# A graph transformer on one core: attention's loop over groups of rows, written out in all five engines

## The chip, the core and the metric

One core of one Trainium2 chip. The time is that of the device, in microseconds (us), of one execution. The core has five engines with an instruction stream each: PE (TensorE, matmuls and their weight loads, which the profile calls PEld), DVE (VectorE), ACT (ScalarE), POOL (GpSimd) and SP (SyncE, which issues the DMAs here). They meet only through semaphores.

## The reference

```python
h = relu(layernorm(x))                                   # x: 1250 x 512, f32
for i in range(4):                                       # L = 4 blocks
    y = cond_layer_norm(h, cond, s1_w[i], ...)
    q, k, v = (y @ wq + bq) * 128 ** -0.5, y @ wk + bk, y @ wv + bv      # 4 heads of 128
    scores = einsum('ehd,ehd->eh', q[src], k[dst])       # 21250 edges
    attn = softmax of the scores over the edges of each src node
    h = h + segment_sum(attn * v[dst], src) @ wo + bo
    y = cond_layer_norm(h, cond, s2_w[i], ...)
    h = h + relu(y @ m_w1 + m_b1) @ m_w2 + m_b2
x = x + h
# then two graph convolutions (GCN) over the same edges with 512 x 512 weights, added to x
```

## The kernel before

The edges are turned at the start into a dense 1250 x 1250 table of counts and a table of its logarithms, the edge bias, kept in memory. Attention is then dense: for a tile of 125 nodes and one head, scores against all 1250 nodes, plus bias, softmax, times V.

The 1250 rows are ten tiles of T = 125, and two tiles make one of NC = 5 **groups**, 0 to 4. A group has UNITS = 8 **units**: 4 heads times 2 tiles, numbered k = 0 to 7. All five engines run a pipeline that is two units deep:

- PE, `unit(G, k)`: `scores` for unit n = k + 2 (9 matmuls into the one score area `ps_S`), then `turn_probs` for unit k (10 transposes of the softmax's output, L1530). After it comes half of `attend` (15 matmuls with V) when k is 2 to 7, all of the last head's (30 matmuls) after k = 0, and `attn_project` (24 matmuls with wo) after k = 1. `scores` waits for two semaphores: `qg` (q is there) and `ttr` (DVE has read the previous unit's scores out of `ps_S`).
- DVE, `unit`: `score_max` for unit n (L1128: one pass of 125x1250 that adds the bias, writes `P` and leaves the row's maximum in `nmx`), `turn_low` for unit k (3 subtractions, L1144), `normalise` for unit n (L1133, L1135 and the scaling L1137). `score_max` waits for three semaphores: `S` (scores are made), `st0` or `st1` (the bias has landed) and `Tp` (PE has transposed the unit before the previous one, so that `P` is free). After odd k comes `out_low` (L1150), and after k = 1 `attn_add` (L1157).
- ACT: exponentials (L757) and copies of the transposes (L763). POOL: splits the next group's q (`q_head`, L516, L519) and adds wo's bias to z (`attn_bias`, L540). SP: loads the next group's q and bias rows.

```python
def scores(G, U, h, u):
    pe.wait_ge(s["qg"], AHEAD + (H * G + h + 1))
    pe.wait_ge(s["ttr"], AHEAD + U)
def score_max(G, U, u, first):
    dve.wait_ge(s["S"], U + 1)
    dve.wait_ge(s[f"st{u}"], 32 * (G + 1))
    if not first:
        dve.wait_ge(s["Tp"], AHEAD + (3 * (U - 1)))
    settled(dve)
```

The four layers are already separate code. Within a layer the first units are written out on every engine, and so is `attn_end`, which does units 2 to 7 of group 4. What lies between is a hardware loop (`Fori`), whose index is a register, and so the values waited for and some addresses are computed in registers. On DVE, ACT, POOL and SP the loop runs 4 times: on DVE it covers `score_max` of units 4 to 7 of group g and 0 to 3 of group g + 1, for g = 0 to 3. On PE it runs 3 times: group 0 up to unit 1 of group 1 is written out, and the loop covers `scores` of units 4 to 7 of group g and 0 to 3 of group g + 1, for g = 1 to 3. The numbering below is that of the unit whose scores or maximum are made.

Of the kernel before, what the change touches and what calls it, by code (L numbers as in the profile page):

```python
# [34 lines left out]
NC = NT // 2  # L35
# [20 lines left out]
def build(nc, x, src, dst, node_vec1, f_w1, f_b1, f_w2, f_b2, s1_w, s1_b, b1_w, b1_b, wq, bq, wk, bk, wv, bv,  # L56
# [5 lines left out]
    with ExitStack() as ctx:  # L62
# [190 lines left out]
        def settled(eng):  # L253

            eng.sem_inc(s["settled"], 1)
# [3 lines left out]
        def _(sp):  # L260
# [61 lines left out]
            def q_view(c):  # L322
                return q_dram[c] if isinstance(c, int) else q_dram[bass.ds(c, 1)].rearrange("a p n -> (a p) n")
# [17 lines left out]
            def bias_row(i):  # L341
                sp.wait_ge(s["bdone"], i + 1)
                move(bias_dram[i * T:(i + 1) * T, :], b_rows[i % 2], f"bst_out{i % 2}")
                if i + 2 < NT:
                    load_counts(i + 2)
# [9 lines left out]
            def layer(l, last, first=False):  # L355
                for i, c in enumerate(PROJECTED[:-1]):
                    sp.wait_ge(s["q_e"], KD * (l * NC + i + 1))
                    sp.dma_start(q_view(c), qc_flat).then_inc(s["q_st"], 16)
                    if first:
                        for t in (2 * i, 2 * i + 1):  # L360
                            bias_row(t)
                sp.wait_ge(s["q_mm"], KD * NC * (l + 1))
                if first:
                    for i in range(2):
                        sp.wait_ge(s[f"bst_out{i}"], 32)
                settled(sp)
                for u in range(2):
                    load_bias(0, u)
                sp.wait_ge(s["q_st"], AHEAD + 16 * (NC - 1) * (l + 1))
                settled(sp)  # L370
                load_output_biases(l)
                if first:
                    for t in (NT - 2, NT - 1):
                        bias_row(t)
                    for i in range(2):
                        sp.wait_ge(s[f"bst_out{i}"], NT * 16)
                    load_o(l)
                    load_m(l)
                sp.wait_ge(s["lnS"], 2 * l + 1)
                settled(sp)  # L380
                load_ln(l, s2_w, s2_b, b2_w, b2_b)
                with sp.Fori(0, NC - 1) as g:
                    G = l * NC + g
                    sp.wait_ge(s["qg"], AHEAD + H * (G + 1))
                    sp.dma_start(qc_flat, q_view(g + 1)).then_inc(s["q_ld"], 16)
                    for u in range(2):
                        sp.wait_ge(s["ttr"], AHEAD + (UNITS * G + UNITS - 1 + u))
                        load_bias(g + 1, u)
                sp.wait_ge(s["ttr"], AHEAD + UNITS * NC * (l + 1))
                settled(sp)  # L390
                load_w(m2r[:, :, :], lay(m_w2, l), "ldM2")
                sp.wait_ge(s["lnS"], 2 * l + 2)
                settled(sp)
                if not last:
                    load_ln(l + 1, s1_w, s1_b, b1_w, b1_b)
                sp.wait_ge(s["PV"], H * NC * (l + 1))
                settled(sp)
                if not last:
                    load_attn(l + 1, wa_raw)
                else:  # L400

                    load_w(wa_raw[:, 0], g_W1, "ldA")
                    sp.dma_start(bvb[:, :], g_b2.rearrange("(a n) -> a n", a=1).to_broadcast([T, D])).then_inc(s["ldA"], 16)
                    load_x(range(8))
                sp.wait_ge(s["zB"], AHEAD + (2 * NC * (l + 1)))
                settled(sp)
                if not last:
                    load_o(l + 1)
                else:
                    load_x(range(8, NT))  # L410
                    load_w(W2[:, :, :], g_W2, "ldG")
                    for t in range(6):
                        move(counts[t], counts_dram[t * T:(t + 1) * T, :], "g_cnt")
                if not last:
                    sp.wait_ge(s["zC"], AHEAD + (2 * NC * (l + 1)))
                    load_m(l + 1)
# [16 lines left out]
        def _(pool):  # L433
            g = nc.gpsimd
# [143 lines left out]
            def layer(l, last):  # L578
                for n in range(NC - 1):
                    cond_chunk(2 * NC * l + n + 1, PROJECTED[n + 1])  # L580
                    v_split(l, n)
                for h in range(H):
                    q_head(l, 0, h)
                v_split(l, NC - 1)
                split_wo(l)
                with pool.Fori(0, NC - 1) as g_:
                    G = l * NC + g_
                    for h in range(H):
                        pool.wait_ge(s["S"], UNITS * G + 2 * h + 2)
                        q_head(l, g_ + 1, h)  # L590
                    attn_bias(l, g_)
                attn_bias(l, NC - 1)
                split_ln(2 * l + 1)
                cond_chunk(2 * NC * l + NC, 0)
                mlp_bias(l, 0)
                cond_chunk(2 * NC * l + NC + 1, 1)
                for c in range(NC):
                    h_low(l, c, (0, 1))
                    if c + 2 < NC:
                        cond_chunk(2 * NC * l + NC + c + 2, c + 2)  # L600
                    h_low(l, c, (2, 3))
                    if c + 2 == NC and not last:
                        split_ln(2 * l + 2)
                        cond_chunk(2 * NC * (l + 1), PROJECTED[0])
                    if c + 1 < NC:
                        mlp_bias(l, c + 1)
                    if last and c > 0:
                        add_x(c - 1)
                    if c == 1:
                        pool.wait_ge(s["wmS"], 2 * l + 2)  # L610
                    if 0 < c < 4 and not (last and c > 1):
                        split_wa(wa_raw, l + 1, c - 1, 0 if last else 3 - c)
# [12 lines left out]
        def _(act):  # L625
# [190 lines left out]
            def layer(l, last, first=False):  # L816
                f = 2 * NC * l
                act.wait_ge(s["zm"], 2 * NC * l)
                for n in range(NC - 1):
                    yT_out(f + n, yT if n % 2 else yTb)  # L820
                    if last and n == 2:
                        degrees()
                    rsqrt0(f + n + 1)
                    q_out(l, n)
                    k_out(l, n)
                    if first:
                        for i in (2 * n, 2 * n + 1):
                            bias_halves(i)
                yT_out(f + NC - 1, yTb)
                q_out(l, NC - 1)  # L830
                k_out(l, NC - 1)
                if first:
                    for i in (NT - 2, NT - 1):
                        bias_halves(i)
                attn_begin(UNITS * NC * l)
                with act.Fori(0, NC - 1) as g_:
                    attn_rest(l * NC + g_)
                    attn_first(l * NC + g_ + 1)
                f2 = 2 * NC * l + NC
                attn_end(l * NC + NC - 1, f2)  # L840
                yT_out(f2)
                split_m(l)
                if last:
                    for c in range(NC):
                        if c:
                            yT_out(f2 + c)
                        rsqrt0(f2 + c + 1)
                        if c == NC - 1:
                            front_relu(0)
                        h_out(l, c)  # L850
                        if c == 1:
                            split_next(l, 0, 0, 32)
                    rsqrt0(f2 + NC + 1)
                    front_relu(1)
                else:
                    for c in range(NC):
                        if c:
                            yT_out(f2 + c)
                        rsqrt0(f2 + c + 1)
                        h_out(l, c)  # L860
                        if c < 3:
                            split_next(l, c, 2 - c, 64)
# [27 lines left out]
        def _(dve):  # L890
# [353 lines left out]
            def layer(l, last, first=False):  # L1244
# [25 lines left out]
                score_max(l * NC, U + 3, 1, False)  # L1270
                normalise(U + 2, 0)
                normalise(U + 3, 1)
                with dve.Fori(0, NC - 1) as g_:
                    attn_rest(l, g_)
                    attn_first(l, g_ + 1)
                f2 = 2 * NC * l + NC
# [71 lines left out]
        def _(pe):  # L1348
# [242 lines left out]
            def layer(l, last):  # L1591
# [8 lines left out]
                pe.wait_ge(s["woS"], l + 1)  # L1600
                settled(pe)
                attn_first(l * NC + 1)
                with pe.Fori(1, NC - 1) as g_:
                    attn_rest(l * NC + g_)
                    attn_first(l * NC + g_ + 1)
                attn_end(l * NC + NC - 1, 2 * NC * l + NC, 2 * l + 1)
# [90 lines left out]
```

## Time and profile before

| | |
|---|---|
| median of 3 runs | 2042.19 us (2035.58 to 2043.1) |
| the profiled execution, its own time | 2044.91 us |
| its span, first to last instruction | 2042.8 us |
| PE busy | 1931.2 us, 95% |
| DVE busy | 1369.0 us, 67% |
| ACT busy, POOL busy | 788.6 us, 498.7 us |
| mean granted PE clock | 0.98 |

Times in the views are microseconds from the span's start. Busy PE counts matmuls whose ends are modelled, so short gaps of PE are better seen in the weight loads (PEld), one of which goes ahead of each matmul.

### The profile page before, as it was taken

Reading aid. Unit: us, or ns where it says so; the run is one execution under the profiler, and the core shown is the slowest. Engines: PE = TensorE matmul, PEld = TensorE weight load, DVE = VectorE, ACT = ScalarE, POOL = GpSimd, SP = SyncE. Lnnn points to the kernel's source line nnn. Section 1 sums busy time; section 2 is a strip of 40 time slices with the busy share of each in tenths; the row PEclk is TensorE's granted clock in tenths of the full one; section 3 lists DMA queues with packets and bytes.
Section 4 is the critical chain, followed back from the end, with each engine's and each line's share of the span. In section 5 each row is a group of like instructions: output and inputs, shape, how many; then the busy total and the mean of one; then the engine's idle time right before and its main releaser. Section 6 shows DMA issues by size and latency. Waiting matters only on the chain. (4 is left out here: it accounts for less than half of the span.)

```text
span 2042.8 us, 33899 instructions
## 1 busy us (share of the span) xinstructions
PE 1931.2 (95%) x11664; PEld 1583.2 (78%) x11664; DVE 1369.0 (67%) x2790; ACT 788.6 (39%) x1525; POOL 498.7 (24%) x561
## 2 busy tenths in 40 slices
PE   5898999999999999999999999999999999999999
PEld 2455888898879889888897898888979988865543
DVE  6877558888775588887655888776578888740111
ACT  2222455555432255554223555442245554340000
POOL 1000243112362411214424212062241121510000
PEclk8999999999999999999999999999999999999999
DMA  4012453110300111202001110211031104210000
GB/s 131 25 49 50 139 155 119 35 35 25 113 17 35 60 36 35 59 25 88 31 31 50 48 57 24 80 34 42 23 83 36 35 25 126 67 49 0 1 21 30
DMA packets 50717, 108.34 MB, mean 53 GB/s; under 512 B 18143, under 2 KB 18195, under 8 KB 50608
## 3 DMA queue, kind: packets, MB, share of 16 engines
q1 hardware_dynamic: 50608, 106.87, 17.8%
q8 instruction: 71, 1.16, 0.2%
q14 instruction: 38, 0.31, 0.0%
HBM read 83.60 MB, written 23.25 MB: 52 GB/s over the span
## 5 line engine op out<-in xcount | busy, mean ns | idle before, releaser
L1437 PE MATMUL ps<-kT,qg 128*125 128x512 f32 (+1 forms) x1440 | 318.2, 366 | 13.8 <-DVE nmx L1128 11.4
L1437 PE MATMUL ps<-PT,V 125*128 125x250 f32 x2400 | 312.7, 284 | 1.6 <-DVE PT L1144 1.6
L1128 DVE CUSTOM_DVE_ANT_0 pbuf<-ps,bt 125x1250 f32<-125x1250 f32 x160 | 233.3, 1458 | 120.3 <-PE ps L1530 106.1
L1437 PEld LDWEIGHTS ps<-kT,qg 128*125 128x125 f32 x1440 | 249.6, 190 | 83.0 <-issue 19.0
L763 ACT ACTIVATE PT<-ps 125x500 fp32r<-125x500 f32 (+1 forms) x480 | 214.4, 520 | 238.3 <-PE ps L1530 238.2
L1437 PEld LDWEIGHTS ps<-PT,V 125*128 125x128 f32 x2400 | 289.5, 190 | 2.9 <-DVE PT L1144 2.9
L757 ACT ACTIVATE pbuf<-pbuf,nmx 125x1250 f32<-125x1250 f32 x160 | 214.9, 1343 | 170.2 <-DVE nmx L1128 170.2
L1144 DVE TENSOR_TENSOR PT<-ps,PT 125x500 fp32r<-125x500 f32 (+1 forms) x480 | 253.3, 583 | 2.0 <-ACT PT L763 1.8
L1530 PE MATMUL ps<-ident,pbuf 125*125 125x125 f32 x1600 | 203.3, 274 | 15.2 <-DVE pbuf L1137 15.2
L1530 PEld LDWEIGHTS ps<-ident,pbuf 125*125 125x125 f32 x1600 | 188.0, 189 | 18.2 <-DVE pbuf L1137 17.5
L516 POOL CAST qg<-qc 128x250 fp32r<-128x250 f32 x80 | 46.4, 580 | 471.7 <-PE ps L1437 469.3
L1137 DVE TENSOR_SCALAR pbuf<-pbuf,rden 125x1250 f32<-125x1250 f32 x160 | 150.3, 939 | 5.6
L1437 PEld LDWEIGHTS ps<-yTb,wa 128*128 128x128 f32 x1152 | 139.4, 193 | 5.5 <-issue 3.9
L1437 PE MATMUL ps<-yTb,wa 128*128 128x250 f32 x1152 | 140.3, 282 | 2.7 <-DVE yTb L1095 2.7
L1437 PE MATMUL ps<-wmS,hT 128*125 128x512 f32 x480 | 130.5, 420 | 7.6 <-POOL hT L576 7.6
L1390 PE MATMUL ps<-oh_src,oh_dst 125*125 125x512 bf16 x558 | 121.7, 369 | 12.6 <-DVE oh_src L969 12.6
L1437 PEld LDWEIGHTS ps<-wmS,hT 128*125 128x125 f32 x480 | 90.1, 197 | 37.7 <-ACT qc L737 9.6
L1390 PEld LDWEIGHTS ps<-oh_src,oh_dst 125*125 125x125 bf16 x558 | 66.7, 143 | 66.5 <-DVE oh_src L969 45.9
L1437 PEld LDWEIGHTS ps<-yT,wmS 128*128 128x128 f32 x960 | 114.1, 189 | 1.9
L1437 PE MATMUL ps<-yT,wmS 128*128 128x250 f32 x960 | 114.4, 278 | 0.0
L528 POOL CAST V<-ztmp 125x512 fp32r<-125x512 f32 x40 | 29.8, 745 | 304.5 <-DVE ztmp L1120 304.5
L1437 PE MATMUL ps<-WOS,outTg 128*125 128x512 f32 x320 | 102.2, 400 | 0.3
(189 smaller groups left out, 2762.6 us busy)
## 6 DMA issues: line engine op xcount, KB each, us to landing
bt<-edge_bias_scratch SPq DMA_DIRECT2D x40, 546.9 KB
q_scratch<-qc SPq DMA_DIRECT2D x16, 500.0 KB, 2.6
qc<-q_scratch SPq DMA_DIRECT2D x16, 500.0 KB, 4.7
counts_scratch<-cblk SPq DMA_DIRECT2D x10, 546.9 KB
c_rows<-counts_scratch SPq DMA_DIRECT2D x10, 546.9 KB
edge_bias_scratch<-b_rows SPq DMA_DIRECT2D x10, 546.9 KB
counts<-counts_scratch SPq DMA_DIRECT2D x10, 546.9 KB
wm<-in_L_gnn_wo_dram SPq DMA_DIRECT2D x4, 1024.0 KB, 8.5
```

The lines of the kernel that those rows point to most:

```text
L516: g.tensor_copy(qg[:, 0, h, :], qc[:, h, :]).then_inc(s["qgh"], 1)
L528: g.tensor_copy(vh, ztmp[:, u, :]).then_inc(s["vhi"], 1)
L757: sc.activation(P[:, u, :], P[:, u, :], ACT.Exp, bias=nmx[:, u:u + 1], scale=-1.0, accum_out=den[:, u:u + 1]).then_inc(s["exp"], 1)
L763: sc.activation(PT[:, h % 2, 0, a:b, u * T:(u + 1) * T], ps_T[0:T, i, 0:(b - a) * T].rearrange("p (t n) -> p t n", n=T), ACT.Copy).then_in ...
L1128: v.tensor_tensor_reduce(out=P[:, u, :], in0=ps_S, in1=bt[:, u, :], scale=-1.0, scalar=FLOOR, op0=ALU.add, op1=ALU.min, accum_out=nmx[:, u ...
L1137: v.tensor_scalar(P[:, u, :], P[:, u, :], rden[:, u:u + 1], None, ALU.mult).then_inc(s["P"], 1)
L1144: v.tensor_tensor(o[:, 1], ps_T[0:T, i, 0:(b - a) * T].rearrange("p (t n) -> p t n", n=T), o[:, 0].bitcast(F32), ALU.subtract).then_inc(s[ ...
L1390: e = mm(psf[0:T, o + a:o + b], oh_dst[:, slot, 0:T], oh_src[:, slot, a:b], start=False, stop=False, skip_group_check=True)
L1437: e = mm(out_, lhs(a), rhs(b), start=start and i == 0, stop=stop and i == 2)
L1530: e = turn(ps_T[0:T, p, (m - a) * T:(m - a + 1) * T], P[:, u, m * T:(m + 1) * T], ident[0:T, 0:T])
```

## The change

Each of the five `Fori` loops over the groups becomes a Python loop: the same instructions, once for each group, with constants in place of registers.

```diff
-                with sp.Fori(0, NC - 1) as g:
+                for g in range(NC - 1):
-                with pool.Fori(0, NC - 1) as g_:
+                for g_ in range(NC - 1):
-                with act.Fori(0, NC - 1) as g_:
+                for g_ in range(NC - 1):
-                with dve.Fori(0, NC - 1) as g_:
+                for g_ in range(NC - 1):
                     attn_rest(l, g_)
                     attn_first(l, g_ + 1)
-                with pe.Fori(1, NC - 1) as g_:
+                for g_ in range(1, NC - 1):
                     attn_rest(l * NC + g_)
                     attn_first(l * NC + g_ + 1)
```

```order
L1273 UNCONDITIONAL_BRANCH
L1273 ISA
L1124 ISA [waits S]
L1126 ISA [waits st0]
L1128 ISA pbuf,nmx<-ps,bt 125x1250 [waits Tp]
L1128 ISA nmx 125x1
L1142 ISA
L1144 TENSOR_TENSOR PT<-ps,PT 125x4x125 [waits Thi]
L1142 REGISTER_ALU
L1144 TENSOR_TENSOR PT<-ps,PT 125x4x125 [waits Thi]
```

And the same place after the change:

```order
L1137 TENSOR_SCALAR pbuf<-pbuf,rden 125x1250 [waits rden]
L1128 ISA pbuf,nmx<-ps,bt 125x1250 [waits Tp,S,st0]
L1128 ISA nmx 125x1
L1144 TENSOR_TENSOR PT<-ps,PT 125x4x125 [waits Thi] x2
L1144 TENSOR_TENSOR PT<-ps,PT 125x2x125 [waits Thi]
```

The register instructions are gone, and with them the rows that carried the waits for S and st0: all three waits now belong to the pass, as they do before the change in the units that were written out already. The second place is PE, units 4 and 5 of group 1, where its loop starts: `scores`, `turn_probs`, half of `attend`, `scores`. Before:

```order
L1603 UNCONDITIONAL_BRANCH
L1603 ISA
L1520 ISA [waits qg]
L1437 MATMUL ps<-kT,qg 125x512 [waits ttr]
L1437 MATMUL ps<-kT,qg 125x512 x5
L1437 MATMUL ps<-kT,qg 125x226 x3
L1526 REGISTER_ALU
L1527 ISA [waits P]
L1530 MATMUL ps<-ident,pbuf 125x125 [waits Te]
L1530 MATMUL ps<-ident,pbuf 125x125 x9
```

And the same place after the change:

```order
L1437 MATMUL ps<-WOS,outTl 125x512
L1437 MATMUL ps<-kT,qg 125x512 [waits ttr,qg]
L1437 MATMUL ps<-kT,qg 125x512 x5
L1437 MATMUL ps<-kT,qg 125x226 x3
L1530 MATMUL ps<-ident,pbuf 125x125 [waits Te,P]
L1530 MATMUL ps<-ident,pbuf 125x125 x9
```

Here too the waits for qg and ttr now stand together ahead of the first score matmul. The order of the matmuls and of DVE's passes is the same on both sides, here and in every other group.

## Rows read from the trace of the kernel before

**Rows 1.** The page: span, busy time of the engines, the instruction queue of DMA
```profile
span 2042.8 us, 33899 instructions
PE 1931.2 (95%) x11664; PEld 1583.2 (78%) x11664; DVE 1369.0 (67%) x2790; ACT 788.6 (39%) x1525; POOL 498.7 (24%) x561
...
q8 instruction: 71, 1.16, 0.2%
```

**Rows 2.** Windows, layer 0: one period of PE's loop (window; length; busy; clock)
```profile
403.30:446.70 43.40, 43.40 (x297) 39.01 (x297) 35.80 (x71) 23.34 (x44) 8.05 (x10) 1.00 0.14 41
```

**Rows 3.** Timeline of PE's weight loads, layer 0, group 2
```profile
387.71 1.80 PEld L1437 LDWEIGHTS ps<-kT,qg 128*125 128x125 f32 x9 [0.17 <-DVE nmx L1128]
```

**Rows 4.** Timeline of DVE, group 1 of layer 0 and group 3 of layer 3
```profile
367.01 1.46 DVE L1128 CUSTOM_DVE_ANT_0 pbuf<-ps,bt 125x1250 f32<-125x1250 f32 x1 [2.08 <-PE ps L1530]
371.80 1.46 DVE L1128 CUSTOM_DVE_ANT_0 pbuf<-ps,bt 125x1250 f32<-125x1250 f32 x1 [0.56 <-PE ps L1530]
...
1650.53 1.46 DVE L1128 CUSTOM_DVE_ANT_0 pbuf<-ps,bt 125x1250 f32<-125x1250 f32 x1 [0.24 <-PE ps L1530]
1655.31 1.46 DVE L1128 CUSTOM_DVE_ANT_0 pbuf<-ps,bt 125x1250 f32<-125x1250 f32 x1 [0.56 <-PE ps L1530]
```

**Rows 5.** Timeline, layer 3: DVE's units 3, 4 of group 1; scores behind PE's branch
```profile
1545.57 1.46 DVE L1128 CUSTOM_DVE_ANT_0 pbuf<-ps,bt 125x1250 f32<-125x1250 f32 x1 [1.78 <-PE ps L1530]
...
1553.95 1.46 DVE L1128 CUSTOM_DVE_ANT_0 pbuf<-ps,bt 125x1250 f32<-125x1250 f32 x1 [2.07 <-PE ps L1530]
...
1594.03 1.91 PEld L1437 LDWEIGHTS ps<-kT,qg 128*125 128x125 f32 x9
```

**Rows 6.** Sequencer instructions of the loops' edges, whole span: ns min/median/max
```profile
L1603 PEldq COMPARE_BRANCH  x12: 76/208/228, 403.2 to 1677.8; - x12
...
L1273 DVEq COMPARE_BRANCH  x16: 50/56/63, 364.3 to 1682.5; - x16
```

**Rows 7.** Timeline, layer 0: units 0, 1 of group 1, then scores of unit 2
```profile
342.58 1.46 DVE L1128 CUSTOM_DVE_ANT_0 pbuf<-ps,bt 125x1250 f32<-125x1250 f32 x1 [0.30 <-PE ps L1530]
...
347.43 1.46 DVE L1128 CUSTOM_DVE_ANT_0 pbuf<-ps,bt 125x1250 f32<-125x1250 f32 x1 [0.62 <-PE ps L1530]
...
349.02 1.80 PEld L1437 LDWEIGHTS ps<-kT,qg 128*125 128x125 f32 x9 [0.23 <-issue]
```

**Rows 8.** Timeline, group 4 of layer 0 (units 4 to 6) and of layer 3
```profile
498.13 1.46 DVE L1128 CUSTOM_DVE_ANT_0 pbuf<-ps,bt 125x1250 f32<-125x1250 f32 x1 [2.18 <-PE ps L1530]
...
503.07 1.46 DVE L1128 CUSTOM_DVE_ANT_0 pbuf<-ps,bt 125x1250 f32<-125x1250 f32 x1 [0.71 <-PE ps L1530]
...
508.04 1.46 DVE L1128 CUSTOM_DVE_ANT_0 pbuf<-ps,bt 125x1250 f32<-125x1250 f32 x1 [0.42 <-PE ps L1530]
...
509.62 1.80 PEld L1437 LDWEIGHTS ps<-kT,qg 128*125 128x125 f32 x9 [0.34 <-issue]
...
1690.11 1.46 DVE L1128 CUSTOM_DVE_ANT_0 pbuf<-ps,bt 125x1250 f32<-125x1250 f32 x1 [0.71 <-PE ps L1530]
...
1695.04 1.46 DVE L1128 CUSTOM_DVE_ANT_0 pbuf<-ps,bt 125x1250 f32<-125x1250 f32 x1 [0.38 <-PE ps L1530]
```

**Rows 9.** Timeline, layer 0: DVE up to units 0 and 1 of group 4; POOL
```profile
471.66 1.62 DVE L1137 TENSOR_SCALAR pbuf<-pbuf,rden 125x1250 f32<-125x1250 f32 x1
...
473.53 1.44 DVE L1128 CUSTOM_DVE_ANT_0 pbuf<-ps,bt 125x1250 f32<-125x1250 f32 x1
...
478.55 1.45 DVE L1128 CUSTOM_DVE_ANT_0 pbuf<-ps,bt 125x1250 f32<-125x1250 f32 x1
...
468.83 5.60 POOL L540 TENSOR_TENSOR z<-z,bob 125x512 f32 x4
```

**Rows 10.** DMA view of the window 403.3 to 446.7: all of its queues
```profile
q1 hardware_dynamic: 452, 1.76, 14.4%
```

**Rows 11.** The same view, window 358 to 403.3 (PE's loop, first time round)
```profile
q8 instruction: 3, 0.05, 0.4%
```

**Rows 12.** Chain of waits summed, whole span: us in total, times, longest
```profile
PEld ps L1437 <- issue: 25.9, 50, 2.0
```

## The prediction

> **What bounds the kernel now.** I read the page first: PE is busy 1931.2 us of 2042.8, DVE only 1369.0 [rows 1]. So work that is taken off DVE, ACT, POOL or SP gains nothing by itself, and the question is what ends PE's waits in the stretch that the loops cover. The windows say how large that stretch is: one period of PE's loop takes 43.4 us, with 43.40 us of modelled matmul time in it, so PE seems never to stop [rows 2]. The weight loads show otherwise. Before the first weight load of each `scores` PE stands idle for 0.17 us, and what it waits for is `nmx`, the end of DVE's pass L1128 [rows 3]. DVE in turn was idle 0.24 to 0.56 us before that pass, until PE's transposes L1530 ended [rows 4]. This is a closed ring: transposes, pass, scores into the one score area, transposes. Its period is the distance between two passes. Both loops run in 60 such intervals of the four layers; the first is 371.80 - 367.01 = 4.79 us, the last 1655.31 - 1650.53 = 4.78 us, and their mean is 4.795 us [rows 4]. PE's half of `attend` lies inside the ring's slack and does not quite fill it, which is the 0.17 us. So in these units the *reaction time* of DVE to a semaphore, and of PE to a semaphore, is on the path.
>
> In two of eight units it is not. Behind unit 2's scores PE has 30 matmuls instead of 15, behind unit 3's the 24 of `attn_project`; DVE then idles about 2 us (1.78 and 2.07) before its pass and the interval is PE's own, 1553.95 - 1545.57 = 8.38 us [rows 5]. The ring decides 6 of 8 intervals in a group.
>
> **What the change removes.** The branches and the register instructions. A branch takes 208 ns on PE (12 of them) and 56 ns on DVE (16) [rows 6]. Are they on the path? Behind PE's branch of layer 3 the next scores' weight loads begin at 1594.03 us with no idle time at all [rows 5]: the sequencer is ahead of the matmuls there. DVE's branch falls into the 2 us in which it waits for PE anyway [rows 5]. ACT, POOL and SP have more slack than these. I cost the removal at nothing; bare of cover it would be 12 x 0.208 + 16 x 0.056 = 3.4 us.
>
> **What it adds.** No work, but another form of waiting. The order shows that in the loop the last semaphore, the one that comes late, stands alone on the pass (Tp) or on the scores (ttr), while the early ones stand on register instructions ahead. Written out, the instruction has three waits, or two. The kernel before holds both forms, so the price can be read from it:
>
> - *PE written out, DVE in its loop* is group 0 up to the scores of unit 3 of group 1. There the interval is 347.43 - 342.58 = 4.85 us and PE's idle time before the scores is 0.23 us in place of 0.17 [rows 7]. PE's price is 4.85 - 4.795 = 0.055 us for each `scores` that waits.
> - *Both written out* is group 4 from unit 4 on. There the intervals are 503.07 - 498.13 = 4.94 and 508.04 - 503.07 = 4.97 us, and PE's idle time 0.34 us [rows 8]. Four layers have eight such intervals, the last of them 1695.04 - 1690.11 = 4.93 us, with a mean of 4.945 us. DVE's price is 4.945 - 4.85 = 0.095 us for each pass.
>
> The passes take 1.46 us in all three, so nothing but the start is late.
>
> **Counting.** Passes that the ring decides: units 4 to 7 of group g and 0, 1 of group g + 1, g = 0 to 3, all of them in DVE's loop now: 24 in a layer. Two of them don't count. Ahead of units 0 and 1 of group 4 DVE has no idle time: its scaling L1137 takes 1.62 us while POOL does four additions in a row, and it ends as the pass begins [rows 9]. A wait that is answered 0.1 us later is hidden behind that. That leaves 22. Scores that wait for `ttr`: six in each of the three groups that PE's loop covers, less the two whose delay ends in those same two passes, 16.
>
> 22 x 0.095 + 16 x 0.055 = 2.09 + 0.88 = 2.97 us in a layer, 11.9 us in four. The profiled execution takes 2044.91 us and would take 2056.8; it lies 2.7 us above the median of the runs shown, 2042.19, from which the same sum gives 2054.1 us, and that is my forecast. If the two hidden passes cost as well, it is 1.2 us more.
>
> **Instruction loading.** In a period of PE's loop the DMA has no queue but the data's [rows 10], where the whole program has 71 transfers for PE's instructions [rows 1]: the loop's body is fetched once and kept. Written out, the two further periods of each layer have to be fetched. The loop's first time round takes 3 of these transfers [rows 11], so at most 2 x 3 x 4 = 24, say 20, are added to 71. The 71 don't show as idle time where PE is written out today: its idle times there, 0.23 and 0.34 us, are the ring's [rows 7, 8]. I cost them at nothing; the bound from above is the mean of PE's unexplained waits, 25.9 / 50 = 0.52 us each [rows 12], 10 us.
>
> The Trainium skill speaks against my forecast. Its page "Runtime: NRT & Kernel Launch", section "Instruction fetch mechanics", says that a taken branch whose target is outside the window of two blocks forces a fetch before execution goes on, and that kernels therefore prefer full unrolling. By that rule this change would gain. The trace does not bear it out here: no instruction transfer falls into the loop's period.
>
> **The rivals.**
> 1. *The loops' edges cost more than they show: faster.* The mechanism is a stall at each branch that is taken, 8 on PE. Priced by the longest unexplained wait of PE, 2.0 us [rows 12], they would give back 16 us, and with no price for the waits the time is 2026; with it 2038. To turn the sign the stall must be over 11.9 / 8 = 1.5 us for each taken branch of PE, and over 2.8 us to be measurably faster. Against it: no idle time behind the branch [rows 5].
> 2. *Only PE's half is true, or only DVE's: no change that can be measured.* Group 4 could be slow for a reason of its own, since ACT and POOL are written out there too. Then PE's 16 x 0.055 x 4 = 3.5 us remain, 2046. With DVE's half alone it is 22 x 0.095 x 4 = 8.4 us, 2051. Against it: the same 0.055 and 0.095 in all layers, and the pass starts late where nothing else does.
> 3. *Instruction loading shows.* 20 transfers at 0.52 us on top, 2064. For it: attention's straight code is now three times as long, and SP's bias loads share the DMA engines. Against it: groups 0 and 4 don't show it.
>
> **Chances and range.** The forecast 0.70, rival 1 0.06, rival 2 0.18, rival 3 0.06. A measurement of this kernel tells changes of over about 0.5%, 10.2 us, from none. The forecast, +11.9 us, is close to that: the three runs before spread by 7.5 us. I give it 3 in 4 to come out beyond. So slower 0.70 x 0.76 + 0.06 = 0.59, same 0.17 + 0.18 = 0.35, faster 0.06. The range takes rival 2 in part and rival 3: 2045 to 2063 us.
>
> **What would show it.** Right: DVE's passes in groups 1 to 3 stand 4.93 to 4.97 us apart where it was 4.79; PE's idle time before the scores is 0.31 to 0.34 us; the interval of 8.38 us stays; PE's loop period of 43.4 us becomes 43.4 + 6 x 0.15 = 44.3; some 20 more instruction transfers. Wrong, if the intervals in groups 1 to 3 stay at 4.8 or go to 4.85 (rival 2), if gaps stand in PE's weight loads in the middle of 15 or 30 matmuls (rival 3), or if the interval of 8.38 us shrinks (rival 1).

## The result, and the profile after

The changed kernel takes 2047.13 us in the median of 20 runs (2042.0 to 2053.57), the one before 2041.64 us in the median of 20 (2035.58 to 2046.8): a ratio of 1.003, 95% interval 1.0019 to 1.0041. It is slower by 5.5 us, where 11.9 were forecast. The profiled execution took 2046.07 us, that of before 2044.91.

The page of the changed kernel (span, busy time, DMA's instruction queues), to be read against [rows 1]:

```profile
span 2044.3 us, 31937 instructions
PE 1921.0 (94%) x11664; PEld 1575.5 (77%) x11664; DVE 1368.0 (67%) x2790; ACT 788.4 (39%) x1525; POOL 498.5 (24%) x561
...
q8 instruction: 90, 1.47, 0.3%
q14 instruction: 48, 0.39, 0.1%
```

The number of matmuls is unchanged, but PE is busy 10.2 us less. The same matmuls took less time, so the clock granted to them must have been higher: its mean is 0.986 in place of 0.98. The prediction has no such line. PE's instruction transfers went from 71 to 90, as forecast.

DVE's passes in group 1 of layer 0, from units 0 and 1 on, where [rows 7] show 4.85 and [rows 5] 8.38 us:

```profile
341.01 1.46 DVE L1128 CUSTOM_DVE_ANT_0 pbuf<-ps,bt 125x1250 f32<-125x1250 f32 x1 [0.39 <-PE ps L1530]
...
345.96 1.46 DVE L1128 CUSTOM_DVE_ANT_0 pbuf<-ps,bt 125x1250 f32<-125x1250 f32 x1 [0.71 <-PE ps L1530]
...
357.23 1.46 DVE L1128 CUSTOM_DVE_ANT_0 pbuf<-ps,bt 125x1250 f32<-125x1250 f32 x1 [1.78 <-PE ps L1530]
...
365.61 1.46 DVE L1128 CUSTOM_DVE_ANT_0 pbuf<-ps,bt 125x1250 f32<-125x1250 f32 x1 [2.29 <-PE ps L1530]
...
370.56 1.46 DVE L1128 CUSTOM_DVE_ANT_0 pbuf<-ps,bt 125x1250 f32<-125x1250 f32 x1 [0.71 <-PE ps L1530]
```

345.96 - 341.01 = 4.95 us, 370.56 - 365.61 = 4.95 where [rows 4] have 4.79, and 365.61 - 357.23 = 8.38 as before. PE's weight loads in layer 0, and the sum of PE's unexplained waits, against [rows 3] and [rows 12]:

```profile
386.98 1.79 PEld L1437 LDWEIGHTS ps<-kT,qg 128*125 128x125 f32 x9 [0.32 <-issue]
```

```profile
PEld ps L1437 <- issue: 55.2, 123, 2.4
```

The idle time ahead of `scores` is 0.32 us where it was 0.17. One period, against [rows 2], forecast at 44.3 us:

```profile
405.15:449.54 44.39, 43.46 (x298) 39.07 (x297) 35.85 (x71) 23.35 (x44) 7.93 (x10) 1.00 0.14 40
```

So in the attention's steady part everything came as forecast, and the time was given back elsewhere. The windows below cut layers 2 and 3 at three passes each: the layer's first, its sixth, its last (window; length; busy of PE, PEld, DVE, ACT, POOL; PE's granted clock; DMA). The middle window of a layer holds the ring; the third is the MLP up to the next layer, after layer 3 the end. Before:

```profile
1094.07:1119.12 25.05, 20.40 (x115) 17.08 (x114) 19.32 (x35) 11.74 (x21) 14.21 (x17) 0.93 0.17 50
1119.12:1305.33 186.21, 184.87 (x1266) 166.32 (x1264) 155.03 (x301) 99.71 (x189) 35.65 (x40) 1.00 0.13 36
1305.33:1489.82 184.49, 177.12 (x1185) 157.98 (x1185) 115.22 (x224) 61.65 (x138) 69.48 (x79) 0.98 0.17 56
1489.82:1514.97 25.15, 20.40 (x115) 17.16 (x114) 19.32 (x35) 11.75 (x21) 14.21 (x17) 0.93 0.19 50
1514.97:1701.21 186.24, 184.89 (x1266) 166.37 (x1264) 155.01 (x300) 99.68 (x189) 35.69 (x40) 1.00 0.13 36
1701.21:2042.78 341.57, 326.03 (x1213) 199.44 (x1211) 115.80 (x227) 62.10 (x126) 46.33 (x49) 0.98 0.17 44
```

After the change:

```profile
1098.73:1121.94 23.21, 19.02 (x116) 16.10 (x115) 18.70 (x36) 11.86 (x21) 15.38 (x17) 1.00 0.18 55
1121.94:1310.88 188.94, 184.69 (x1265) 166.21 (x1263) 154.91 (x301) 99.64 (x189) 35.25 (x40) 1.00 0.13 36
1310.88:1492.89 182.01, 174.63 (x1185) 155.88 (x1185) 115.64 (x224) 61.46 (x138) 69.44 (x79) 1.00 0.17 56
1492.89:1517.94 25.05, 20.31 (x116) 17.44 (x115) 19.43 (x36) 11.98 (x21) 14.01 (x17) 0.93 0.16 51
1517.94:1706.78 188.84, 184.68 (x1265) 166.22 (x1263) 154.91 (x301) 99.66 (x189) 35.21 (x40) 1.00 0.13 36
1706.78:2044.30 337.52, 323.27 (x1212) 197.12 (x1211) 116.01 (x227) 61.86 (x126) 46.36 (x49) 0.99 0.16 44
```

The ring's windows grew by 2.73 and 2.60 us. The window behind layer 2 went from 184.49 to 182.01 us while its clock went from 0.98 to 1.00; the end from 341.57 to 337.52 with 0.98 to 0.99; layer 2's start from 25.05 to 23.21 with 0.93 to 1.00. Those windows also hold changes that are not the clock's: in layer 2's start the first two intervals are 1.0 us shorter (explained below) and the fourth is 0.5 us longer. Layer 3's start, with 0.93 on both sides, kept its length within 0.1 us. Over the whole trace the four ring windows add up to 744.77 us before and 755.87 after, +11.1; everything else to 1298.01 and 1288.43, -9.6.

PE's clock stands at the full 2.4 GHz in nearly all of attention, and falls to 1.2 GHz in the program's first 208 us and then, mostly for 3.4 or 6.8 us each time, at the starts of layers and around the MLP, where PE is idle in parts: before the change it is busy for 177.12 of the 184.49 us behind layer 2, and for 184.87 of the 186.21 us of that layer's ring. Outside the ring these stretches add up to 80.5 us before and 56.5 us after. What a microsecond at the lower level costs can be read at one place. Between the third and the fourth pass of a layer there are 3.8 us when no such stretch falls there (layers 0 and 2 after), and 5.05 to 5.3 us in all four layers of before, with 3.4 us of it (layer 2: 5.17): 1.4 us for 3.4. 24 us less of it at that price are an estimated 10 us, about all of the -9.6. But half-clock time varies between executions of one kernel (the mean clock of a single run of the changed kernel lies between 0.982 and 0.989), so one trace against another doesn't settle how much of this is the change's.

### The profile page after: what moved, and what is told of

It is laid out like the page before. It is cut to its first block and busy times, and to the rows that moved or that the text cites. A ratio compares the mean times of both kernels' runs of the same rounds, so it can differ in the third digit from the quotient of the medians.

```text
span 2044.3 us, 31937 instructions
## 1 busy us (share of the span) xinstructions
PE 1921.0 (94%) x11664; PEld 1575.5 (77%) x11664; DVE 1368.0 (67%) x2790; ACT 788.4 (39%) x1525; POOL 498.5 (24%) x561
## 5 line engine op out<-in xcount | busy, mean ns | idle before, releaser
L1437 PE MATMUL ps<-kT,qg 128*125 128x512 f32 (+1 forms) x1440 | 311.4, 361 | 27.9 <-DVE nmx L1128 24.4
L1128 DVE CUSTOM_DVE_ANT_0 pbuf<-ps,bt 125x1250 f32<-125x1250 f32 x160 | 233.4, 1459 | 133.3 <-PE ps L1530 121.6
L1137 DVE TENSOR_SCALAR pbuf<-pbuf,rden 125x1250 f32<-125x1250 f32 x160 | 148.2, 927 | 5.6
```

The lines of the kernel that those rows point to most:

```text
L1128: v.tensor_tensor_reduce(out=P[:, u, :], in0=ps_S, in1=bt[:, u, :], scale=-1.0, scalar=FLOOR, op0=ALU.add, op1=ALU.min, accum_out=nmx[:, u ...
L1137: v.tensor_scalar(P[:, u, :], P[:, u, :], rden[:, u:u + 1], None, ALU.mult).then_inc(s["P"], 1)
L1437: e = mm(out_, lhs(a), rhs(b), start=start and i == 0, stop=stop and i == 2)
```

## The experiments

Each ratio is to the kernel before, timed beside it on the same chip, with its 95% interval. "Ring" is the sum of the four ring windows in the profiled execution (before: 744.77 us), "half clock" the time at 1.2 GHz outside them (before: 80.5 us).

### The two kernels again

**b_again**, the kernel before under another name, no edit:

> The kernel before once more, for the spread of its time and of its mean granted clock. After the change every interval of the ring grew as forecast (4.79 to 4.95 us), yet the time grew by 5.5 us and not 11.9; the profile after has a mean granted clock of 0.986, that of before 0.980. Theory 1 (clock): the kernel before runs at a lower mean clock than the one after, and the difference gives back some 6 us; the mean clock of before is then 0.979 to 0.983 in most runs. Theory 2 (chance of one profile): both kernels run at the same mean clock, 0.984 to 0.986, and the missing 6 us are work or waits elsewhere. Ratio to before 1.000 +- 0.002 by both.

Measured: 1.0 (0.9989 to 1.001), ring 744.5 us, half clock 80.5 us. **a_again**, the changed kernel once more:

> The kernel after once more, on the same chip. Ratio 1.002 to 1.004 by all theories. Theory 1 (clock): its mean clock lies above that of the kernel before by 0.003 to 0.005, and at equal clock it is 11 to 12 us longer. Theory 2: equal clocks, and at equal clock it is only 5 to 6 us longer.

Measured: 1.0015 (1.0005 to 1.0025), ring 755.7 us, half clock 67.0 us; mean clock over the runs 0.9858, against 0.9818 of before. The small slowdown is real, though a little under the 1.002 expected, and so is the long ring in it. The measurement resolves about 0.1%. The mean clock differs by 0.004, as the first of the two theories had it.

### Each half of the ring alone

**pe_only**:

```diff
-                with pe.Fori(1, NC - 1) as g_:
+                for g_ in range(1, NC - 1):
```

> Only PE's loop is written out; the other four stay loops. By the forecast's count the ring's intervals in groups 1 to 3 go from 4.795 to 4.85 us, 16 x 0.055 = 0.9 us in a layer, 3.5 us in all at equal clock. If the price is not PE's wait form but something of group 0's, the intervals stay at 4.795. Time against before: +1 to +4 us (0.05 to 0.2%).

Measured: 0.9997 (0.9987 to 1.0007), ring 748.6 us. **dve_only**:

```diff
-                with dve.Fori(0, NC - 1) as g_:
+                for g_ in range(NC - 1):
```

> Only DVE's loop is written out. By the forecast's count DVE's passes start 0.095 us later each: intervals of 4.89 us in groups 1 to 3 and 4.945 in groups 0 and 4, where PE is written out too; 22 x 0.095 = 2.1 us in a layer, 8.4 us in all at equal clock. Theory 1 (clock) lets some of it come back through a higher mean clock: +4 to +8 us. If rival 2 held (only PE's form costs) the intervals would stay at 4.795.

Measured: 1.0017 (1.0009 to 1.0026), ring 751.8 us. Two neighbouring passes in group 2, of pe_only and then of dve_only:

```profile
415.07 1.46 DVE L1128 CUSTOM_DVE_ANT_0 pbuf<-ps,bt 125x1250 f32<-125x1250 f32 x1 [0.62 <-PE ps L1530]
419.92 1.46 DVE L1128 CUSTOM_DVE_ANT_0 pbuf<-ps,bt 125x1250 f32<-125x1250 f32 x1 [0.29 <-PE ps L1530]
```

```profile
414.20 1.46 DVE L1128 CUSTOM_DVE_ANT_0 pbuf<-ps,bt 125x1250 f32<-125x1250 f32 x1 [0.65 <-PE ps L1530]
419.08 1.46 DVE L1128 CUSTOM_DVE_ANT_0 pbuf<-ps,bt 125x1250 f32<-125x1250 f32 x1 [0.32 <-PE ps L1530]
```

4.85 and 4.88 us in place of 4.79: PE's half costs 0.06 us an interval and DVE's about 0.09. In the ring's sums they are +3.8 and +7.1 us, and the prediction's two terms were 3.5 and 8.4. The times are less: medians of -0.2 and +3.4 us, each some 4 us below its ring sum, though ACT, POOL and SP kept their loops in both. Here too the mean clock is higher, 0.985 and 0.984 against 0.9818 of before on that chip.

### Is it the writing out, or where the late wait stands?

**loop_late** keeps all five loops. In DVE's loop only, `score_max` waits for Tp, the one that comes late, first. A register instruction then carries that wait, and the instruction that waits for S and st stands between it and the pass:

```diff
 def score_max(G, U, u, first):
+    if not first and not isinstance(U, int):
+        dve.wait_ge(s["Tp"], AHEAD + (3 * (U - 1)))
     dve.wait_ge(s["S"], U + 1)
     dve.wait_ge(s[f"st{u}"], 32 * (G + 1))
-    if not first:
+    if not first and isinstance(U, int):
         dve.wait_ge(s["Tp"], AHEAD + (3 * (U - 1)))
```

> The kernel before with all five loops kept; only in DVE's loop the wait for Tp now comes first in the source, so that a register instruction carries it and one more wait instruction stands between it and the pass. If the place of the wait is the price and writing out is not, the intervals of groups 1 to 3 go from 4.795 to 4.88 us as in the run in which only DVE's loop was written out, +2.1 us in a layer, +8.4 in all at equal clock, and the time comes out at 2044 to 2049. If writing out itself were the price, nothing changes.

Measured: 1.0037 (1.0022 to 1.0053), ring 755.4 us. DVE in group 1 (the edit moved the lines by two):

```profile
375.29 1.46 DVE L1130 CUSTOM_DVE_ANT_0 pbuf<-ps,bt 125x1250 f32<-125x1250 f32 x1 [0.35 <-PE ps L1532]
380.20 1.46 DVE L1130 CUSTOM_DVE_ANT_0 pbuf<-ps,bt 125x1250 f32<-125x1250 f32 x1 [0.69 <-PE ps L1532]
```

4.91 us, with no loop written out. That is more than the 4.88 expected, and so is the ring's +10.6 us against the 8.4. **written_swapped** is the opposite: all five written out, and the late wait put last, next to the work:

```diff
 def scores(G, U, h, u):
-    pe.wait_ge(s["qg"], AHEAD + (H * G + h + 1))
     pe.wait_ge(s["ttr"], AHEAD + U)
+    pe.wait_ge(s["qg"], AHEAD + (H * G + h + 1))
 def score_max(G, U, u, first):
-    dve.wait_ge(s["S"], U + 1)
-    dve.wait_ge(s[f"st{u}"], 32 * (G + 1))
     if not first:
         dve.wait_ge(s["Tp"], AHEAD + (3 * (U - 1)))
+    dve.wait_ge(s["S"], U + 1)
+    dve.wait_ge(s[f"st{u}"], 32 * (G + 1))
```

In the code the late wait now comes first. In the built program the order of two waits that stand together is turned: the wait written first is carried by the work or by the instruction next to it, and the later ones by instructions ahead.

> The kernel after, with the two or three waits in another order in the source, so that the late semaphore stands next to the work: PE waits for ttr on the first score matmul and for qg ahead of it; DVE waits for Tp in the last instruction before its pass and for st0 or st1 ahead. Nothing else differs. If the price is the place of the late wait, the ring's intervals fall from 4.945 to 4.80 us in all groups, 0 and 4 too: 30 intervals in a layer at 0.15 us, 4 us in a layer, some 16 us against after and 4 us against before at equal clock. Theory of the clock: the mean clock falls back to about 0.982, and the time comes out at 2040 to 2044, no gain that can be measured. If writing out costs by itself (constants, code loading), the intervals stay at 4.94.

Measured: 2031.92 us, 0.9959 (0.9945 to 0.9974), ring 743.6 us. PE and DVE in layer 0, then:

```profile
387.19 1.78 PEld L1437 LDWEIGHTS ps<-kT,qg 128*125 128x125 f32 x9 [0.20 <-DVE nmx L1128]
391.99 1.80 PEld L1437 LDWEIGHTS ps<-kT,qg 128*125 128x125 f32 x9 [0.17 <-DVE nmx L1128]
```

```profile
414.82 1.46 DVE L1128 CUSTOM_DVE_ANT_0 pbuf<-ps,bt 125x1250 f32<-125x1250 f32 x1 [0.59 <-PE ps L1530]
419.63 1.46 DVE L1128 CUSTOM_DVE_ANT_0 pbuf<-ps,bt 125x1250 f32<-125x1250 f32 x1 [0.25 <-PE ps L1530]
```

4.81 us with everything written out, and PE's idle time is back at 0.17 to 0.20. The forecast of 2040 to 2044 us was missed: it let the mean clock fall back to 0.982, and it was 0.9862 against 0.9840 of before.

The trace shows the price directly. The order listings of the change put all waits of a pass or of a first matmul on that one instruction. In the trace of the changed kernel some stand on instructions of their own ahead of it, on DVE and on PE:

```profile
L1126 DVEq EVENT_SEMAPHORE  x152: 21/21/21, 311.7 to 1706.0; - x152
L1520 PEldq EVENT_SEMAPHORE  x160: 51/51/51, 294.6 to 1702.1; - x160
```

By the semaphores in the trace's records, these two carry the late waits, Tp and ttr. On DVE a second instruction of 50 ns, with the waits for S and st, stands between the first and the pass. Before the change, in the loops, Tp stands on the instruction right ahead of the pass, and ttr on the weight load itself. The table gives the median time from the event of the late semaphore to the start of the work, for 52 passes of groups 1 to 3 that the ring decides and for the 118 to 121 loads that begin within 0.6 us of ttr:

| | Tp to the pass | ttr to the first weight load |
|---|---|---|
| before | 182 ns | 42 ns in PE's loop, 104 where it is written out |
| after | 273 ns | 104 ns |
| written_swapped | 204 ns | 42 ns |
| loop_late | 292 ns | as before |

The differences are the intervals': 91 and 62 ns after the change, 22 ns on DVE in written_swapped (4.81 and not 4.79), 110 ns on DVE in loop_late (4.91). Together the two runs decide it: the ring's price hangs on which instruction carries the wait that is answered last, not on the loops. **loop_best** keeps the loops and turns the waits only in the units that were written out already (the same two swaps, where `U` is a Python integer):

> The kernel before with its loops; in the parts that are written out already (group 0 of PE, group 4 of both) the late wait stands next to the work. Intervals of groups 0 and 1 fall from 4.85 to 4.80 and of group 4 from 4.945 to 4.80: some 8 x 0.055 + 3 x 0.15 = 0.9 us in a layer, 3.5 us at equal clock. By the theory of the clock part of it may be taken back: -4 to 0 us against before.

Measured: 0.9975 (0.9964 to 0.9986), ring 741.9 us, the shortest of all; the ring's intervals in groups 0 and 4 are, but for one, 4.78 to 4.83 us in place of 4.83 to 4.97. The time fell by 5 us where the ring's sum fell by 2.9; the runs don't say where the rest lies.

### The other three engines

**others_written**: PE's and DVE's loops are kept, and the three others are written out:

```diff
-                with sp.Fori(0, NC - 1) as g:
+                for g in range(NC - 1):
-                with pool.Fori(0, NC - 1) as g_:
+                for g_ in range(NC - 1):
-                with act.Fori(0, NC - 1) as g_:
+                for g_ in range(NC - 1):
```

> Only the loops of SP, POOL and ACT are written out; PE's and DVE's stay. None of the three is on the ring by its waits for PE or DVE, so intervals stay at 4.795, and the time at that of before, 2041 to 2044, mean clock 0.982. If ACT's or POOL's form costs or gains something, the intervals move.

Measured: 0.9974 (0.9962 to 0.9986), ring 745.0 us. The ring is unchanged and yet the kernel is 6 us faster, against every forecast of mine. So it was repeated on another chip:

> The kernel with ACT, POOL and SP written out once more, on this chip: 0.9965 to 0.9985 if its gain of 0.26% was real, 0.9995 to 1.0005 if it was the chip's or the round's.

Measured: 2035.13 us, 0.9975 (0.9962 to 0.9988). The complement, on that same chip, is **ring_written**, PE's and DVE's loops written out and the three others kept:

> Only PE's and DVE's loops are written out; ACT, POOL and SP keep theirs. If the gain of the kernel with the three others written out (0.9974) is theirs alone, this kernel lacks it and is slower than the fully written-out one: the ring's 11 us, less what fewer microseconds at the half clock give back, 2 to 5: ratio 1.003 to 1.0045. Rival: that gain was only a kinder place of the half-clock stretches, which the longer ring brings anyway; then this kernel equals the fully written-out one, 1.0015 to 1.003, with a mean clock of 0.985 to 0.986. Ring intervals 4.94 to 4.96 either way.

Measured: 2052.55 us against 2041.09, 1.005 (1.003 to 1.0069), ring 755.9 us, mean clock 0.9834, just that of before on that chip (0.9834). By the medians the ring's half is +11.5 us, the other half -6.0 us, and their sum +5.5 us is what the whole change measured. That the sum fits to the decimal is luck: the intervals reach from 6 to 14 us and from -8 to -2.5 us. Nor do the parts of the ring's half add up: pe_only and dve_only multiply to 1.0014, not 1.005, and what differs is the mean clock, which rose in those two and did not rise here. **ring_swapped** is ring_written with the waits of written_swapped:

> PE and DVE written out with the early wait last, next to the work, ACT, POOL and SP in their loops. Ring intervals 4.80 to 4.82. If the gain of 0.4% of the fully written-out version with these waits came from the three other engines, this kernel is at 0.999 to 1.0005 with the clock of before; if it came from the ring's waits in the units that were written out before already, it is at 0.996 to 0.998.

Measured: 0.9978 (0.9966 to 0.999), ring 743.5 us. The turned waits make up more than the loops' price, since they also serve the units that were written out before. Written_swapped is 0.2% below it, on another chip. That fits the three other engines' share, but the two intervals overlap.

### Which of the three, and how?

Of the three lines above, only ACT's, only POOL's, only SP's:

> Only ACT's loop is written out. The ring's intervals stay at 4.80. If ACT is what made the kernel with the three others written out faster, the ratio is 0.997 to 0.9985 here; if it is POOL or SP, it is 0.9995 to 1.0005 and the mean clock stays near 0.982. Layer 2's first units tell the same: 4.48 and 4.67 us apart if ACT does it, 4.71 and 5.48 if not.

Measured: 0.9989 (0.9978 to 1.0), mean clock 0.9843.

> Only POOL's loop is written out. If POOL is what gives back, the first three intervals of layer 2 are 4.48, 4.67 and 3.79 us in place of 4.71, 5.48 and 5.2, and the ratio is 0.997 to 0.9985. If it is SP, or the three together, the intervals stay and the ratio is 0.9995 to 1.0005.

Measured: 0.9984 (0.9973 to 0.9995), mean clock 0.9853 against 0.9841 of before.

> Only SP's loop is written out. Layer 2's first intervals stay at 4.71, 5.48 and 5.0 to 5.3 us and the ratio is 0.9995 to 1.0005 if POOL is what gives back; 0.997 to 0.9985 if SP does, through loads that are issued at another time.

Measured: 0.9999 (0.9989 to 1.0009). The three ratios multiply to 0.9972, against 0.9974 and 0.9975 together. POOL's part is the largest by the medians; ACT's interval ends at no change, and POOL's holds ACT's ratio, so the order of the two isn't shown.

One microsecond of POOL's part has a mechanism that the traces show, at layer 2's start. DVE's scaling L1137 and POOL's cast and additions get in each other's way, and whoever comes first goes at its own pace. Before (DVE, then POOL):

```profile
1097.71 1.15 DVE L1137 TENSOR_SCALAR pbuf<-pbuf,rden 125x1250 f32<-125x1250 f32 x1
...
1102.73 1.62 DVE L1137 TENSOR_SCALAR pbuf<-pbuf,rden 125x1250 f32<-125x1250 f32 x1
1097.59 0.61 POOL L528 CAST V<-ztmp 125x512 fp32r<-125x512 f32 x1 [2.50 <-DVE ztmp L1120]
...
1102.42 3.06 POOL L552 TENSOR_TENSOR WOS<-wm,WOS 128x512 fp32r<-128x512 f32 x2 [0.18 <-POOL WOS L547]
```

After the change:

```profile
1102.37 0.88 DVE L1137 TENSOR_SCALAR pbuf<-pbuf,rden 125x1250 f32<-125x1250 f32 x1
...
1107.10 0.87 DVE L1137 TENSOR_SCALAR pbuf<-pbuf,rden 125x1250 f32<-125x1250 f32 x1
1102.53 1.18 POOL L528 CAST V<-ztmp 125x512 fp32r<-125x512 f32 x1 [2.80 <-DVE ztmp L1120]
...
1107.48 2.88 POOL L552 TENSOR_TENSOR WOS<-wm,WOS 128x512 fp32r<-128x512 f32 x2 [0.18 <-POOL WOS L547]
```

Before, the cast begins 0.12 us ahead of the scaling, and the scaling takes 1.15 us. After, it begins 0.16 us behind it; now the scaling takes 0.88 and the cast 1.18 in place of 0.61. The next scaling comes ahead of POOL's additions instead of behind them, and takes 0.87 in place of 1.62. The first two intervals of the layer go from 4.71 and 5.49 us to 4.48 and 4.68: 1.0 us. In every kernel in which POOL is written out this happens in layer 2, and in none of those that keep POOL's loop except the one below, which forces it; in pe_only, dve_only, act_written and ring_written the intervals are 4.71 and 5.48. The Trainium skill's page "SBUF — State Buffer", section "Who interferes with whom", says that the order of issue decides which of the two engines blocks on the port they share; the trace agrees, with 1.15 and 0.61 us one way and 0.88 and 1.18 the other. Why POOL's cast starts 0.3 us later (its idle time is 2.80 in place of 2.50), and in layer 2 alone, I could not see: no transfer or semaphore accounts for it.

**port_first** makes that order on purpose in all four layers, with all loops kept:

```diff
 def v_split(l, n, us=range(2)):
     for u in us:
+        if n == NC - 1 and u == 1:
+            pool.wait_ge(s["P"], UNITS * NC * l + 1)
```

> The kernel before with one wait more on POOL in each layer: its cast of the last V tile waits until DVE has scaled unit 0. If DVE's scaling is long because POOL works beside it, the first scaling takes 0.87 us in all four layers and the first intervals are 4.48, 4.7 and 3.8 us in all four: 1.6 to 2.4 us less in each layer, 6 to 9 us in all, ratio 0.9955 to 0.997. If the half clock moves in behind it, half of that is lost: 0.9975. If the order of the two is not the cause, the intervals stay at 4.71, 5.48, 5.2 and the ratio is 0.9995 to 1.001.

Measured: 0.9996 (0.9986 to 1.0007). DVE and then POOL at layer 1's start:

```profile
698.84 0.87 DVE L1139 TENSOR_SCALAR pbuf<-pbuf,rden 125x1250 f32<-125x1250 f32 x1
...
703.58 1.20 DVE L1139 TENSOR_SCALAR pbuf<-pbuf,rden 125x1250 f32<-125x1250 f32 x1
699.90 0.61 POOL L530 CAST V<-ztmp 125x512 fp32r<-125x512 f32 x1 [3.70 <-DVE pbuf L1139]
```

The first interval is 4.48 to 4.53 us in all four layers, so the order is the cause of that one. But the second is 5.0 us in place of 5.5, not 4.7, since the scaling still meets POOL (1.20), and in layer 0 it grew from 5.4 to 6.15. Over the four layers the first two intervals are 1.5 us shorter in sum, which the interval of the ratio neither shows nor excludes, and the forecast of 0.9955 to 0.997 was missed. **best_port** is written_swapped with this wait:

> All five loops written out, the late wait next to the work, and POOL's wait of port_first. Ring intervals 4.80 to 4.82 and first intervals 4.48, 4.7, 3.8 in every layer. If both gains add: 0.996 less 0.002 to 0.003, so 0.993 to 0.994; if the wait brings nothing: 0.996.

Measured: 2030.26 us against 2039.52, 0.9953 (0.9935 to 0.997). It is the fastest version of the study, but its interval holds written_swapped's 0.9959; that the wait adds anything isn't shown.

### What the rest of the six microseconds is

The shift at layer 2's start is 1.0 us. The rest shows as clock. Over the 18 profiled executions (before, after, 16 experiments) the time outside the ring windows follows the half-clock time in it: a straight line through the 18 points is 1262.7 us plus 0.44 us for each microsecond at half clock, with a correlation of 0.97 and no point off it by more than 1.8 us. It agrees with the 1.4 us for 3.4 at a layer's start (0.41). Over many runs the mean clock is 0.9860 and 0.9859 in the two timings with the three engines written out, 0.9840 and 0.9834 before on the same chips. By the runs of before on these two chips, 0.001 of mean clock goes with 1.5 to 1.6 us, so that is 3 to 4 us. Together with the 1.0 us it is most of the 6.

The same estimate, with 1.5 us for each 0.001 (the four chips' runs of before give 1.25 to 1.7), brings the kernels to equal clock:

| against before | mean time of the runs | mean clock | at equal clock (estimate) | ring |
|---|---|---|---|---|
| pe_only | -0.5 us | +0.0032 | +4.4 us | +3.8 us |
| dve_only | +3.4 us | +0.0022 | +6.8 us | +7.1 us |
| loop_late | +7.8 us | +0.0019 | +10.6 us | +10.6 us |
| ring_written | +10.6 us | +0.0001 | +10.7 us | +11.1 us |
| a_again | +3.0 us | +0.0040 | +8.9 us | +11.0 us |
| others_written, others_again | -5.1, -5.3 us | +0.0020, +0.0026 | -2.0, -1.5 us | +0.2 us |

So at equal clock the ring's sum is nearly the whole of the loops' price on PE and DVE, and little more than the 1.0 us is left of the three other engines' gain. The clock's share is no property of these three: it is largest among the parts in pe_only, which leaves them alone.

Why there is less half-clock time is not settled. The stretches stand at the borders of attention and the MLP in all kernels, and at a given border they are there in one execution and absent in the next. A kernel with POOL's loop kept can have it too (loop_late: 0.9858, pe_only: 0.985), and one with all the ring's delay does not (ring_written: 0.9834). No experiment here moved the clock by design.

## Why the prediction was half right

- **"This is a closed ring", and what bounds it.** Right. PE's and DVE's edits moved its intervals, and at equal clock the time moved by nearly the ring's sum; the edits of ACT, POOL and SP left it at 744.7 to 745.2 us.
- **DVE's price of 0.095 and PE's of 0.055 us.** Right: the intervals that the ring decides are 4.94 and 4.95 us in nearly all groups, 4.85 and 4.88 with one half alone. From the semaphore to the work it is 0.091 and 0.062 us.
- **The count and the sum of 11.9 us.** Right for the ring: +11.1 us in the trace, +11.5 in ring_written's time (6 to 14 by its interval). The small rest went at places that the sum had left out: where DVE's loop ended, the interval from unit 7 to 0 fell from 5.23 to 5.07 us, and group 4's from unit 3 to 4 from 8.49 to 8.38.
- **The form of waiting as the cause.** Right, and sharper now: not the number of waits on one instruction, as the order listings suggest, but the instructions that stand between the late wait and the work. loop_late has the price without writing out, written_swapped writes out without the price.
- **"ACT, POOL and SP have more slack than these. I cost the removal at nothing", and "work that is taken off DVE, ACT, POOL or SP gains nothing by itself".** This is the step that failed: the term put at nothing measured -6 us, 0.25%, in two timings. Slack in busy time was the wrong question, because none of it comes from work taken off. In layer 2 POOL's instruction starts elsewhere against DVE's, and the two share a resource: 1.0 us. The rest is granted clock outside the ring, 3 to 4 us by estimate, and what raised it stays open.
- **Adding the ring's 11.9 us to the profiled time as it was.** The same fault from the other side: it assumed the remaining 1298 us of the kernel to stay as they are at the same granted clock. It measured 1288.43 us, 9.6 less, with 24 us less at half clock. 0.01 of mean clock goes with 13 to 17 us here, more than the whole effect, and the prediction had no term for it. It names the spread of the three runs before, 7.5 us, and does not ask where that comes from.
- **Instruction loading.** 19 transfers more on PE, as forecast (20), with no gap in the middle of PE's weight loads. PE's unexplained waits rose by 29.3 us (25.9 to 55.2), but 73 of them are new (50 to 123), 0.40 us each, and as many waits for `nmx` (72, 15.0 us) are gone from the list: they are the ring's own idle times, counted there before. That writing out gains by itself was not seen on PE and DVE: pe_only and dve_only were 0.9997 and 1.0017.
- **The rivals.** The first, loops' edges: refuted for PE and DVE, since ring_written gains nothing. The second, that only one half is true: refuted, since pe_only and dve_only each lengthen the ring; the time came near its 2046 to 2051 for another reason. The third: not seen.
- **Ranges and chances.** The measured 2047.13 us lies in the range, near its low end, where it was put for rival 2, so that it lies there is luck. A change of 0.3% is "same" by the bound of 0.5%, to which I gave 0.35 against 0.59 for slower.

## What to carry to other kernels

When an instruction has several waits, find the one that is answered last and see in the built program which instruction carries it: 0.06 us on PE and 0.09 on DVE, paid on 88 passes and 64 scores, made 11 us. Turning the order of two or three lines took 0.7% off the kernels with PE and DVE written out (1.003 to 0.9959, 1.005 to 0.9978) and 0.25% off the one with its loops. An engine with slack is not one whose edits cost nothing: ask what shares a resource with it at that moment, and test the "nothing" by a run with that edit alone, as soon as the forecast is a per cent or less. And compare granted clock and length window by window before reading a total, since a few hundredths of clock in the windows that the change doesn't touch can hide half of a real effect.

## What the runs showed of the hardware that was not expected

- Two instructions of DVE and POOL that meet delay each other by who is first: scaling 0.88 and cast 1.18 us, or 1.15 and 0.61.
- A few of DVE's passes are 0.35 us late where DVE is written out, three in a run of the changed kernel, at the same places in its repetition and in ring_written. In layer 0 of the changed kernel:

```profile
395.66 1.46 DVE L1128 CUSTOM_DVE_ANT_0 pbuf<-ps,bt 125x1250 f32<-125x1250 f32 x1 [0.76 <-PE ps L1530]
...
401.63 1.46 DVE L1128 CUSTOM_DVE_ANT_0 pbuf<-ps,bt 125x1250 f32<-125x1250 f32 x1 [1.42 <-PE ps L1530]
```

  The idle time is 0.76 us in place of 0.39, and as the next interval is 5.97 in place of 6.33, nothing is lost here; in ring intervals it is. Instruction transfers would fit: q14's went from 38 to 48, or to 44 with DVE alone written out, and in the changed kernel, its repetition and ring_written one of them begins 0.48 to 0.65 us after the start of each of these passes. That they are the cause was not tried.
- A loop's branch takes 208 ns on PE in the median [rows 6], and writing the loop out gained nothing: there was no idle time behind the branch [rows 5].
- A wait carried by an instruction of its own delays the work by 62 ns on PE and, with one more instruction in between, by 91 ns on DVE (the table of semaphore events above).
